# Projecting and rotating the keys of a batch element in one set of 128 rows, with their gap from a matmul and the first loads in another order

## The chip, the cores and the metric

The kernel runs on one core of a Trainium2 chip. The metric is the device time of one execution in microseconds, the median of three runs. One further execution was taken by the hardware profiler; all rows below come from it, with times from the start of its span.

## What is computed

One transformer layer over 4 batch elements of 1024 tokens and 256 features, in fp32: attention with 16 query heads and 4 key/value heads of 16 features, rotary embedding on queries and keys, then a gated feed-forward part, each with residual and layer norm. Only the start of it matters here:

```python
q = (hidden_states @ wq).reshape(B, S, H, D)
k = (hidden_states @ wk).reshape(B, S, Hkv, D)
v = (hidden_states @ wv).reshape(B, S, Hkv, D)
q = q * cos + _rotate_half(q) * sin
k = k * cos + _rotate_half(k) * sin
...
scores = jnp.einsum('bqkgd,bskd->bkgqs', qg, k) * scale
attn = jax.nn.softmax(scores, axis=-1)
```

## The kernel before

The five engines run programs written out by hand, ordered against each other by semaphores. There are three stages: projections, attention, feed-forward. The change is in the first.

**Projections.** The 4096 tokens are 8 blocks `m` of 512; two blocks make a batch element `b`, and `c` is the block within it. For each block TensorE (PE) runs six hooks `h`: two query halves `j` of two steps each (`project_q`, L1160, 128 output rows), and two steps for keys and values (`project_kv`, L1170). The block's 128 key/value rows are 64 of keys and 64 of values; which comes first alternates with `c`. One fp32 matmul appears in the trace as two instructions. VectorE (DVE) multiplies the query rows by the cosine and sine tables (L697, four products a block) and the key rows likewise (L705 to L707, three products of 64, 32 and 32 rows a block). GpSimd (POOL) adds or subtracts the products (`rotate`, L533). ScalarE (ACT) rounds each result to a high part (L959), and POOL, or DVE for the first query half of blocks 0 to 4, takes the rest as the low part (L522, L714). SyncE (SP) stores high and low parts in DRAM tensors `q_parts` and `k_parts`. For each batch element the difference of the rotated keys of its two blocks, the **gap**, is computed by DVE (L720) or, for the last two, POOL (L543), split the same way and stored too.

**Early maxima.** From block 5 on, PE adds in each hook two matmuls of the first attention unit (`max_block`, L1121), through a ring of PSUM banks: ACT takes one of a pair (L992, `above`) and DVE the other (L742). After block 7 the rest of them follows in a row. The row maxima of the first half unit are transposed by PE (`split`), split by DVE (L754, L756) and written by SP into `q_sb` (`load_shift`, L351); only then can the first scores (L1256) run.

**The queue of SP.** It is one ordered list. Inputs: `load_x(m)` loads block m of x. In block m SP waits for each high and low part before it stores it, and everything behind waits too. `load_x(m + 2)` stands after the two stores of the first query half of block m. `first_loads` (the operands of the first maxima, read back from DRAM) stands in block 3 behind the stores of that half, and first waits for all stores of batch element 0, its gap among them.

**The start.** SP issues x(0), wq, wkv (192 columns, since the key columns stand in it twice), both query tables whole, x(1), both key tables, x(2), the identity. PE waits for x(0), wq and wkv; DVE waits for all four tables.

Of the kernel before, what the change touches and what calls it, by code (L numbers as in the profile page):

```python
# [13 lines left out]
P = 128  # L14
CH = 512
# [23 lines left out]
GAPS = 2  # L39
# [5 lines left out]
QK = 3  # L45
PARTS = (3, 4, 7)
# [11 lines left out]
def layer(nc, x, xT, wq, wkv, wo, gate_w, gate_scale, up_w, up_scale, down_w, down_scale,  # L58
          cos, sin_q, cos_k, sin_k, identity, out):
    ctx = ExitStack()  # L60
    with ctx:
# [25 lines left out]
        wq_sb, wkv_sb = sb("wq_sb", [P, KE, E], fp32, one), sb("wkv_sb", [P, KE, 3 * HKV * D], fp32, one)  # L87
        cos_sb, sinq_sb = sb("cos_sb", [P, S], fp32, one), sb("sinq_sb", [P, S], fp32, one)
        cosk_sb, sink_sb = sb("cosk_sb", [P, CH], fp32, one), sb("sink_sb", [P, CH], fp32, one)
        by_cos = [sb(f"by_cos{c}", [P, CH], fp32, one) for c in range(QK)]  # L90
        by_sin = [sb(f"by_sin{c}", [P, CH], fp32, one) for c in range(QK)]
        v_rows = [sb(f"v_rows{c}", [P, CH], fp32, one) for c in range(2)]
        rotated = [sb(f"rotated{c}", [P, CH], fp32, one) for c in range(QK)]
        rotated_k = [rotated[QK - 1], sb("rotated_k1", [P, CH], fp32, one)]
        gap = sb("gap", [HKV * D, CH], fp32, one)
        gap_h, gap_l = sb("gap_h", [HKV * D, CH], f32r, one), sb("gap_l", [HKV * D, CH], f32r, one)
        high = [sb(f"high{c}", [P, CH], f32r, one) for c in range(2 * QK)]
        low = [sb(f"low{c}", [P, CH], f32r, one) for c in range(2 * QK)]
# [62 lines left out]
        kv_bank = [ring_bank[2], pv_bank]  # L161


        proj_loaded, consts_loaded = sem("proj_loaded"), sem("consts_loaded")
# [4 lines left out]
        lo_ready = [sem(f"lo_ready{j}") for j in range(QK)]  # L169
        stored = [sem(f"stored{c}") for c in range(2 * QK)]  # L170
        gap_ready, gap_h_ready, gap_l_ready, gap_stored = (sem(n) for n in ("gap_ready", "gap_h_ready", "gap_l_ready", "gap_stored"))
# [52 lines left out]
        for b in range(B):  # L224
            early[min(2 * b + 3, BLOCKS), 1].append(("v", b))
        for i in range(2 * LEAD):
            n, h = divmod(FIRST * HOOKS + i, HOOKS)
            where = early[(n, h) if n < BLOCKS else (BLOCKS, HOOKS - 1)]
            if i == 2 * KT + 1:
                where.append((0, "split"))  # L230
            where.extend(step(i))
        for n in range(BLOCKS + 1):
            if n == BLOCKS:
                wide_from = len(readers)
            for h in range(HOOKS):
                for key in early[n, h]:
                    place(key, "v" if key[0] == "v" else "max" if key[1] == "split" else ("above" if blocks(key[0], key[1] // 4)[key[1] % 4][1] == 2 else "max"))
# [20 lines left out]
        ring_taken = {"max": (ring_used, 1), "above": (above_ready, 1), "v": (v_used, 2)}  # L258
# [36 lines left out]
        def stores(slot):  # L295

            return 16 * 2

# [26 lines left out]
        def _(sp):  # L325
# [7 lines left out]

            load_x(0)
# [18 lines left out]
            def first_loads():  # L353

                for slot in range(2 * QK):
                    sp.wait_ge(stored[slot], stores(slot))
# [5 lines left out]
            def projections(b, first, last):  # L362
                for c in range(2):
                    cols = slice(c * CH, (c + 1) * CH)
                    for j in range(QK):
                        if j == 2 and c == 0 and not first:
                            store_gap(b - 1)
                        if j == 1 and 2 < 2 * b + c + 2 < BLOCKS:
                            load_x(2 * b + c + 2)
                        if b == 3 and c == 0 and j == 1:  # L370
                            load_kv(0, 0)
                            load_k(k_max, 0, 1, kmax_loaded, sp)
                            load_q(0, QH, sp)
                        if b == 1 and c == 1 and j == 1:
                            first_loads()
                        if b == 2 and c == 0 and j == 2:
                            load_q(0, 1, sp)
                        if last and c == 1 and j == 1:
                            load_shift(0, 0, taken_through((0, "split")))
                        slot = QK * c + j  # L380
                        for part, buf, ready, count in ((0, high, hi_ready, 2 * QK * b + slot + 1), (1, low, lo_ready[j], 2 * b + c + 1)):
                            sp.wait_ge(ready, count)
                            if j < 2:
                                dst = q_parts[H * b:H * (b + 1), part, j * HALF:(j + 1) * HALF, cols]
                                sp.dma_start(dst, buf[slot][:].bitcast(fp32)).then_inc(stored[slot], 16)
                            else:
                                store_k(part, b, cols, buf[slot], stored[slot])

            def store_k(part, b, cols, buf, done):
                dst = k_parts[b, part * D:(part + 1) * D, :, cols].rearrange("r h t -> (r h) t")  # L390
                sp.dma_start(dst, buf[0:HKV * D, :].bitcast(fp32)).then_inc(done, 16)

            def store_gap(b):
                for part, buf, ready in ((0, gap_h, gap_h_ready), (1, gap_l, gap_l_ready)):
                    sp.wait_ge(ready, b + 1)
                    store_k(part, b, slice(S, S + CH), buf, gap_stored)
# [32 lines left out]
            for slot in range(2 * QK):  # L429
                sp.wait_ge(stored[slot], stores(slot) * B)  # L430
# [75 lines left out]
        def _(pool):  # L506
# [9 lines left out]
            def low_part(n, slot, j, guard):  # L516
                rows = P if j < 2 else HKV * D
                if guard is not None:
                    pool.wait_ge(*guard)
                pool.wait_ge(hi_ready, n + 1)  # L520
                src = rotated[j] if j < 2 else rotated_k[slot // QK]
                pool.tensor_tensor(low[slot][0:rows], src[0:rows], high[slot][0:rows].bitcast(fp32), ALU.subtract).then_inc(lo_ready[j], 1)  # L522

            def rotate(m, j):
                b, c = divmod(m, 2)
                rows = P if j < 2 else HKV * D
                pool.wait_ge(parts_ready, PARTS[-1] * m + PARTS[j])
                if m:
                    pool.wait_ge(lo_ready[j], m if j < 2 else m - 1)
                if j == QK - 1 and b:  # L530
                    pool.wait_ge(gap_ready, b)
                dst = rotated[j] if j < 2 else rotated_k[c]
                pool.tensor_tensor(dst[0:rows], by_cos[j][0:rows], by_sin[j][0:rows], ALU.add if j else ALU.subtract).then_inc(rot_ready, 1)  # L533

            def low_of(m, j):
                b, c = divmod(m, 2)
                slot = QK * c + j
# [876 lines left out]
```

## Time and profile before

| | us |
|---|---|
| median of 3 runs (lowest to highest) | 948.05 (947.54 to 948.25) |
| the profiled execution's own time | 946.2 |
| its span | 944.0 |
| PE busy in the span | 909.5 (96%) |
| DVE busy | 761.7 (81%) |
| ACT busy | 720.3 (76%) |
| POOL busy | 263.1 (28%) |

The shares are averages over stages with different limits. The stage that is changed ends in the trace at the first scores, 91 us after the start.

### The profile page before, as it was taken

Reading aid. Unit: us, or ns where it says so; the run is one execution under the profiler, and the core shown is the slowest. Engines: PE = TensorE matmul, PEld = TensorE weight load, DVE = VectorE, ACT = ScalarE, POOL = GpSimd, SP = SyncE. Lnnn points to the kernel's source line nnn. Section 1 sums busy time; section 2 is a strip of 40 time slices with the busy share of each in tenths; the row PEclk is TensorE's granted clock in tenths of the full one; section 3 lists DMA queues with packets and bytes.
Section 4 is the critical chain, followed back from the end, with each engine's and each line's share of the span. In section 5 each row is a group of like instructions: output and inputs, shape, how many; then the busy total and the mean of one; then the engine's idle time right before and its main releaser. Section 6 shows DMA issues by size and latency. Waiting matters only on the chain.

```text
span 944.0 us, 15638 instructions
## 1 busy us (share of the span) xinstructions
PE 909.5 (96%) x5520; PEld 467.6 (50%) x5520; DVE 761.7 (81%) x1522; ACT 720.3 (76%) x938; POOL 263.1 (28%) x223
## 2 busy tenths in 40 slices
PE   7688999999999999999999999999999999999995
PEld 3234334344434444343434444444435888888884
DVE  4787899999999999999999999999973456655544
ACT  1356888989898898988998889888887555555564
POOL 5777366110001001001000100400101666656454
PEclk9797999999999999999999999999999999999998
DMA  6797633133131232213313123221110201101001
GB/s 206 205 266 199 140 89 93 44 85 72 44 72 45 58 76 69 51 43 74 82 45 68 49 51 84 68 52 42 33 52 14 69 24 46 45 26 42 24 23 47
DMA packets 44288, 68.85 MB, mean 73 GB/s; under 512 B 12592, under 2 KB 22832, under 8 KB 44208
## 3 DMA queue, kind: packets, MB, share of 16 engines
q1 hardware_dynamic: 43344, 64.67, 26.1%
q0 software_dynamic: 864, 3.15, 1.1%
q8 instruction: 46, 0.75, 0.3%
q14 instruction: 34, 0.28, 0.1%
HBM read 46.80 MB, written 16.25 MB: 67 GB/s over the span
## 4 chain that ended last, share of the span: by engine, by line
PE 86%; issue 4%; POOL 3%; DVE 2%; ACT 2%; DMA 1%; SPq 0%; POOLq 0%; DVEq 0%; ACTq 0%
PE pv_bank L1198 27%; PE ring_bank L1121 25%; PE pair_bank L1256 13%; PE pair_bank L1319 12%; PE pv_bank L1328 3%; PE ring_bank L1328 3%; PE ring_bank L1208 2%; POOL rotated L533 1%; POOL low L522 1%; ACT probs L1048 1%; PE ring_bank L1134 1%; PE ring_bank L1223 1%; POOL rotated_k L533 0%; DVE v_all L863 0%; DVE low L714 0%
## 5 line engine op out<-in xcount | busy, mean ns | idle before, releaser
L1048 ACT ACTIVATE probs<-pair_bank 128x1024 f32<-128x1024 f32 x512 | 496.4, 1026 | 68.2 <-PE pair_bank L1256 66.9
L745 DVE TENSOR_REDUCE block_max<-ring_bank 128x1 f32<-128x512 f32 x732 | 469.1, 683 | 33.3 <-PE ring_bank L1121 25.6
L1121 PE MATMUL ring_bank<-k_max,q_sb 48*128 48x512 f32 x1003 | 315.4, 476 | 4.6 <-DMA q_sb<-shift 2.2
L1198 PE MATMUL pv_bank<-probs,v_all 128*32 128x512 f32 x2048 | 273.6, 606 | 0.5 <-ACT probs L1048 0.5
L1121 PEld LDWEIGHTS ring_bank<-k_max,q_sb 48*128 48x128 f32 x1003 | 136.6, 185 | 252.1 <-DVE block_max L745 125.3
L1256 PE MATMUL pair_bank<-q_sb,k_sb 50*128 50x512 f32 x1024 | 204.4, 415 | 0.9 <-ACT probs L1048 0.9
L608 POOL TENSOR_TENSOR attn<-attn,inv_rows 128x1024 f32<-128x1024 f32 x7 | 16.7, 2379 | 489.2 <-DMA inv_rows<-inv_d 489.2
L906 DVE SCALAR_TENSOR_TENSOR hid<-pair_bank,up_s,silu 128x512 f32<-128x512 f32 x64 | 47.9, 748 | 86.7 <-ACT silu L1088 86.7
L1256 PEld LDWEIGHTS pair_bank<-q_sb,k_sb 50*128 50x128 f32 x1024 | 101.5, 187 | 32.8 <-ACT probs L1048 14.4
L650 POOL TENSOR_TENSOR hid_l<-hid,hid_h 128x512 fp32r<-128x512 f32 x64 | 82.9, 1295 | 87.8 <-ACT hid_h L1074 87.2
L742 DVE CUSTOM_DVE_ANT_0 above<-ring_bank,above 128x512 f32<-128x512 f32 x136 | 93.8, 692 | 10.5 <-ACT above L992 6.7
L992 ACT ACTIVATE above<-ring_bank 128x512 f32<-128x512 f32 x135 | 80.6, 599 | 6.5 <-PE ring_bank L1121 4.4
L1088 ACT ACTIVATE silu<-pair_bank,gate_s 128x512 f32<-128x512 f32 x64 | 43.7, 683 | 47.5 <-PE pair_bank L1319 47.3
L1198 PEld LDWEIGHTS pv_bank<-probs,v_all 128*32 128x32 f32 x2048 | 40.4, 108 | 74.0 <-issue 73.2
L1074 ACT ACTIVATE hid_h<-hid 128x512 fp32r<-128x512 f32 x64 | 40.3, 629 | 43.1 <-DVE hid L906 43.1
L1160 PE MATMUL pair_bank<-attn,wq_sb 128*128 128x512 f32 x64 | 38.4, 730 | 16.4 <-DMA attn<-xT 9.7
L1319 PE MATMUL pair_bank<-x1T_h,gate_h 128*128 128x512 f32 x128 | 41.1, 402 | 0.3 <-DVE hid L906 0.3
L1319 PE MATMUL pair_bank<-x1T_l,gate_h 128*128 128x512 f32 x128 | 40.5, 397 | 0.0
L1319 PE MATMUL pair_bank<-x1T_h,up_h 128*128 128x512 f32 x128 | 40.3, 396 | 0.0
L1319 PE MATMUL pair_bank<-x1T_l,up_h 128*128 128x512 f32 x128 | 40.3, 396 | 0.0
L959 ACT ACTIVATE high<-rotated 128x512 fp32r<-128x512 f32 (+1 forms) x20 | 12.6, 629 | 35.9 <-POOL rotated L533 35.9
L1328 PE MATMUL pv_bank<-down_h,hid_h 128*128 128x256 f32 x128 | 33.7, 284 | 1.9 <-POOL hid_l L650 1.6
(126 smaller groups left out, 873.4 us busy)
## 6 DMA issues: line engine op xcount, KB each, us to landing
q_sb<-q_parts SPq DMA_DIRECT2D x64, 128.0 KB, 3.3
k_max<-k_parts SPq DMA_DIRECT2D x32, 192.0 KB, 3.8
attn<-xT SPq DMA_DIRECT2D x8, 512.0 KB, 5.5
q_parts<-high SPq DMA_DIRECT2D x16, 256.0 KB, 3.5
q_parts<-low SPq DMA_DIRECT2D x16, 256.0 KB, 3.6
q_sb<-q_parts SPq DMA_DIRECT2D x64, 64.0 KB, 3.4
k_sb<-k_parts SPq DMA_DIRECT2D x32, 128.0 KB, 2.7
attn<-pv_sb SPq DMA_DIRECT2D x128, 32.0 KB
```

The costliest lines, as they stand in the source:

```text
L650: pool.tensor_tensor(hid_l[:, it, :], hid[it % 2][:], hid_h[:, it, :].bitcast(fp32), ALU.subtract).then_inc(hid_l_ready, 1)
L742: dve.tensor_tensor_reduce(out=buf[:], in0=bank, in1=buf[:], scale=1.0, scalar=-3.0e38, op0=ALU.add, op1=ALU.max, accum_out=block_max[half ...
L745: dve.reduce_max(block_max[half % 2][:, col:col + 1], bank, axis=AX.X).then_inc(ring_used, 1)
L906: dve.scalar_tensor_tensor(out=hid[it % 2][:], in0=pair_bank[it % 2][:, 1, :], scalar=up_s[:, it:it + 1], in1=silu[it % 2][:], op0=ALU.mul ...
L992: act.activation(above[(count - 1) % 2][:], bank_of(key), ACT.Relu).then_inc(above_ready, 1)
L1048: act.activation(probs[t % 2][:, 2 * pr:2 * pr + 2, :], pair_bank[pr][:], ACT.Exp, scale=D ** -0.5).then_inc(probs_ready, 1)
L1088: act.activation(silu[it % 2][:], pair_bank[it % 2][:, 0, :], ACT.Silu, scale=gate_s[:, it:it + 1]).then_inc(silu_ready, 1)
L1121: pe.matmul(bank, q_sb[k][rows, i, qt * P:(qt + 1) * P], k_max[k // QH][rows, kind * CH:(kind + 1) * CH], start=True, stop=True).then_inc( ...
L1198: ins = pe.matmul(pv_bank[32 * j:32 * j + 2 * D, :], v_all[:, head, t, :], probs[t % 2][:, 2 * (j % 2) + j // 2, :], start=(t == 0), stop= ...
L1256: ins = pe.matmul(pair_bank[pr][:, r, :], k_sb[s][rows, t * P:(t + 1) * P], q_sb[k][rows, pr, :], start=True, stop=True)
L1319: ins = pe.matmul(pair_bank[it % 2][:, u, :], w[:, k, it * P:(it + 1) * P], v[c][:, k, :], start=(q == 0), stop=(q == len(terms) - 1))
L1328: ins = pe.matmul(sum_bank[t // 2][:, (t % 2) * E:(t % 2 + 1) * E], v[:, k, t * P:(t + 1) * P], w[:, k, :], start=(k == 0 and t % 2 == 0 a ...
```

## The change

What it does:

- **Keys of a batch element in one bank.** `project_kv` now issues four matmuls of 32 output rows per step where one of 128 stood. The keys of both blocks of a batch element land in one bank of 128 rows (`k_bank`), the values of both in another (`v_bank`). Within a block the four strips go to the two banks in turn. DVE rotates the keys once per batch element (three products, of 128, 64 and 64 rows), POOL adds them once (`rotate_k`), ACT and POOL make one high and one low part of 128 rows, and SP stores them in four transfers per batch element of two x 32 rows, where it was two transfers per block. ACT copies the values once per batch element.
- **The gap by a matmul.** `key_signs`, +1 and -1 from the identity, multiplies the rotated keys on PE (`make_gap`, fp32, 64 output rows of 512) into a bank of the ring. ACT and DVE (always DVE now) split it from there. It stands in the last but one hook of the next batch element's first block, and for the last batch element behind the last early maximum.
- **Loads.** SP issues wq, x(0), the first half of both query tables, wkv (128 columns), the key tables, x(1), the second halves, x(2), the identity. PE waits at first for x(0) and wq only, DVE for each table at its first use. `load_x(m + 3)` stands where `load_x(m + 2)` stood, but x(5) comes behind `first_loads`, which moves from block 3 into block 2. The 12 loads of block 6 move ahead of that block's first stores.

```diff
-            load_x(0)
-            for dst, src in ((wq_sb, wq), (wkv_sb, wkv)):
-                sp.dma_start(dst[:], src.rearrange("(k p) n -> p k n", p=P)).then_inc(proj_loaded, 16)
-            for dst, src in ((cos_sb, cos), (sinq_sb, sin_q)):
-                sp.dma_start(dst[:], src).then_inc(consts_loaded, 16)
+            sp.dma_start(wq_sb[:], wq.rearrange("(k p) n -> p k n", p=P)).then_inc(wq_loaded, 16)
+            load_x(0)
+            load_q_tables(0)
+            sp.dma_start(wkv_sb[:], wkv.rearrange("(k p) n -> p k n", p=P)).then_inc(wkv_loaded, 16)
+            for dst, src in ((cosk_sb, cos_k), (sink_sb, sin_k)):
+                sp.dma_start(dst[:], src).then_inc(k_tables_loaded, 16)
             load_x(1)
-            for dst, src in ((cosk_sb, cos_k), (sink_sb, sin_k)):
-                sp.dma_start(dst[:], src).then_inc(consts_loaded, 16)
+            load_q_tables(1)
             load_x(2)
...
+            def projections(b, first, last):
+                for c in range(2):
+                    m = 2 * b + c
+                    if last and c == 0:
+                        load_kv(0, 0)
+                        load_k(k_max, 0, 1, kmax_loaded, sp)
+                        load_q(0, QH, sp)
+                    store_q(m, 0)
+                    if c == 0 and not first:
+                        store_gap(b - 1)
+                    if m + 3 < BLOCKS and m != 2:
+                        load_x(m + 3)
+                    if last and c == 1:
+                        load_shift(0, 0, taken_through((0, "split")))
+                    store_q(m, 1)
+                    if m == 2:
+                        first_loads()
+                        load_x(m + 3)
+                    if m == 4:
+                        load_q(0, 1, sp)
+                    if c == 1:
+                        store_k(b)
...
             def project_kv(m, k):
 
-                c = m % 2
-                if k == 0 and m > 1:
-                    pe.wait_ge(parts_ready, PARTS[-1] * (m - 1))
-                    pe.wait_ge(v_rows_ready, m - 1)
-                ins = pe.matmul(kv_bank[c][:], wkv_sb[:, k, HKV * D * c:HKV * D * (c + 2)], x_in[m][:, k, :], start=(k == 0), stop=(k == KE - 1))
+                b, c = divmod(m, 2)
+                if k == 0 and m == 0:
+                    pe.wait_ge(wkv_loaded, 16)
+                if k == 0 and c == 0 and b:
+                    pe.wait_ge(k_parts_ready, K_PARTS * b)
+                    pe.wait_ge(v_rows_ready, b)
+                for strip in range(4):
+                    a, other = strip // 2, strip % 2 != c
+                    col = (HKV * D if other else 0) + a * STRIP
+                    rows = slice(strip * STRIP, (strip + 1) * STRIP)
+                    ins = pe.matmul((v_bank if other else k_bank)[rows, :], wkv_sb[:, k, col:col + STRIP], x_in[m][:, k, :], start=(k == 0), stop=(k == KE - 1))
                 if k == KE - 1:
                     ins.then_inc(proj_ready, 1)
+
+            def make_gap(b):
+
+                pe.wait_ge(signs_ready, 1)
+                pe.wait_ge(k_rot_ready, b + 1)
+                bank = free_bank(("gap", b))
+                pe.matmul(bank[0:HKV * D, :], key_signs[:].rearrange("p a x -> p (a x)"), rotated_k[:], start=True, stop=True).then_inc(ring_ready, 1)
```

Three places in the order. The first is SP's queue behind the stores of the first gap, before the change; the `attn<-xT` in it is x(5).

```order
L391 DMA k_parts<-gap_h 64x512 [waits gap_h_ready]
L391 DMA k_parts<-gap_l 64x512 [waits gap_l_ready]
L391 DMA k_parts<-high2 64x512 [waits hi_ready]
L391 DMA k_parts<-low2 64x512 [waits lo_ready2]
L385 DMA q_parts<-high3 16x8x512 [waits hi_ready]
L385 DMA q_parts<-low3 16x8x512 [waits lo_ready0]
L332 DMA attn<-xT 128x2x512
L319 DMA k_max0<-k_parts 32x1536 [waits stored4,stored5,stored3,gap_stored,stored2,memsets,stored1,stored0]
L320 DMA k_max0<-k_parts 16x1536
```

The same place after the change, where the `attn<-xT` is again x(5).

```order
L395 DMA k_parts<-gap_l 64x512 [waits gap_l_ready]
L381 DMA q_parts<-high1 16x8x512 [waits hi_ready]
L381 DMA q_parts<-low1 16x8x512 [waits lo_ready1]
L324 DMA k_max0<-k_parts 32x1536 [waits k_stored0,stored3,gap_stored,stored2,memsets,stored1,stored0]
L325 DMA k_max0<-k_parts 16x1536
L324 DMA k_max0<-k_parts 32x1536
L325 DMA k_max0<-k_parts 16x1536
L315 DMA q_sb0<-q_parts 32x2x512
L316 DMA q_sb0<-q_parts 16x2x512
L315 DMA q_sb0<-q_parts 32x2x512
L316 DMA q_sb0<-q_parts 16x2x512
L337 DMA attn<-xT 128x2x512
```

x(5) stood ahead of the wait for the gap's store and of the eight loads; now it stands behind them, but all of it comes a block earlier.

The second place is PE's program at the end of the stage, before the change: the last two early maxima, the first two of the attention stage, and the first scores.

```order
L1121 MATMUL ring_bank<-k_max,q_sb 128x512 [waits above_ready]
L1121 MATMUL pair_bank<-k_max,q_sb 128x512 [waits above_ready]
L1121 MATMUL ring_bank<-k_max,q_sb 128x512 [waits shift_loaded0,memsets,kv_loaded0,v_used,parts_ready]
L1121 MATMUL ring_bank<-k_max,q_sb 128x512 [waits ring_used]
L1256 MATMUL pair_bank<-q_sb,k_sb 128x512 [waits ring_used]
```

And after the change.

```order
L1139 MATMUL ring_bank<-k_max,q_sb 128x512 [waits above_ready]
L1139 MATMUL pair_bank<-k_max,q_sb 128x512 [waits above_ready]
L1205 MATMUL pair_bank<-rotated_k,key_signs 64x512 [waits ring_used,k_rot_ready,signs_ready]
L1139 MATMUL ring_bank<-k_max,q_sb 128x512 [waits memsets,shift_loaded0,v_used,kv_loaded0,v_rows_ready,ring_used,k_parts_ready,parts_ready]
L1139 MATMUL ring_bank<-k_max,q_sb 128x512 [waits above_ready]
L1291 MATMUL pair_bank<-q_sb,k_sb 128x512 [waits gap_l_ready,ring_used]
```

The gap's matmul has come in ahead, and the first scores wait for DVE to have taken the gap's low part out of its bank.

## Rows read from the trace of the kernel before

**Rows 1.** The page's first line.

```profile
span 944.0 us, 15638 instructions
```

**Rows 2.** Busy time by stretch; engines, granted clock, DMA share, GB/s.

```profile
0.00:92.48 92.48, 70.39 (x170) 29.42 (x170) 65.36 (x120) 39.51 (x71) 66.05 (x57) 0.90 0.75 219
92.48:790.00 697.52, 695.79 (x4493) 311.83 (x4492) 612.18 (x1184) 595.87 (x722) 109.47 (x82) 1.00 0.25 62
...
40.00:50.00 10.00, 7.88 (x12) 3.13 (x12) 5.94 (x8) 2.06 (x5) 5.87 (x6) 0.68 0.97 262
```

**Rows 3.** Waits of PE up to 95 us: total, times, longest.

```profile
PE pair_bank L1160 <- DMA attn<-xT: 9.7, 3, 4.5
...
PE ring_bank L1121 <- DMA q_sb<-shift: 2.2, 1, 2.2
PE ring_bank L1121 <- DMA q_sb<-q_parts: 2.2, 1, 2.2
```

**Rows 4.** PE in order of time: start, duration, instruction, count, idle before.

```profile
6.72 6.46 PE L1160 MATMUL pair_bank<-attn,wq_sb 128*128 128x512 f32 x8 [6.72 <-DMA wkv_sb<-wkv]
13.01 1.88 PE L1170 MATMUL ring_bank<-attn,wkv_sb 128*128 128x512 f32 x4
...
41.43 6.17 PE L1160 MATMUL pair_bank<-attn,wq_sb 128*128 128x512 f32 x8 [4.34 <-DMA attn<-xT]
...
50.15 1.98 PE L1160 MATMUL pair_bank<-attn,wq_sb 128*128 128x512 f32 x4 [0.84 <-DMA attn<-xT]
...
61.14 1.12 PE L1160 MATMUL pair_bank<-attn,wq_sb 128*128 128x512 f32 x2
...
70.37 1.12 PE L1160 MATMUL pair_bank<-attn,wq_sb 128*128 128x512 f32 x2
71.85 1.12 PE L1160 MATMUL pair_bank<-attn,wq_sb 128*128 128x512 f32 x2
...
80.62 0.49 PE L1121 MATMUL pair_bank<-k_max,q_sb 48*128 48x512 f32 x1
```

**Rows 5.** DVE's and POOL's first work on the projections.

```profile
12.54 0.13 DVE L685 MEMSET block_max<- 128x32 f32 x2 [12.54 <-DMA sink_sb<-sin_k]
...
14.74 2.50 POOL L533 TENSOR_TENSOR rotated<-by_cos,by_sin 128x512 f32<-128x512 f32 x2 [8.17 <-DVE by_sin L697]
```

**Rows 6.** SP's queue in order of time.

```profile
44.18 0.59 SPq L332 DMA_DIRECT2D attn<-xT  x1
...
45.09 0.38 SPq L319 DMA_DIRECT2D k_max<-k_parts  x1
...
48.32 0.43 SPq L311 DMA_DIRECT2D q_sb<-q_parts  x1
```

**Rows 7.** DMA issues up to 60 us: count, size, from issue to landing.

```profile
attn<-xT SPq DMA_DIRECT2D x7, 512.0 KB, 5.4
...
wq_sb<-wq SPq DMA_DIRECT2D x1, 256.0 KB, 4.2
...
k_parts<-gap_l SPq DMA_DIRECT2D x2, 128.0 KB, 4.9
...
wkv_sb<-wkv SPq DMA_DIRECT2D x1, 192.0 KB, 4.9
```

**Rows 8.** The chain that ended last, in the attention stage.

```profile
99.02 0.99 PE pv_bank L1198 x8
```

**Rows 9.** ACT in block 7.

```profile
77.97 0.63 ACT L959 ACTIVATE high<-rotated 64x512 fp32r<-64x512 f32 x1 [2.03 <-POOL rotated L533]
```

**Rows 10.** SP, PE and DVE at the end of the stage.

```profile
86.20 2.87 SPq L351 DMA_DIRECT2D q_sb<-shift  x4
...
87.43 0.79 PE L1121 MATMUL pair_bank<-k_max,q_sb 48*128 48x512 f32 x1
...
89.06 0.69 DVE L742 CUSTOM_DVE_ANT_0 above<-pair_bank,above 128x512 f32<-128x512 f32 x1
...
91.00 0.66 PE L1256 MATMUL pair_bank<-q_sb,k_sb 50*128 50x512 f32 x2
```

More of the change, by code:

```diff
@@ L44 @@
 STORES = 16 * (G + 1)
-QK = 3
-PARTS = (3, 4, 7)
+Q_PARTS = 4
+K_PARTS = 3
+STRIP = HKV * HALF
+K_STORES = 2
 LAG = 2
@@ L224, in layer @@
         for b in range(B):
+            if b < B - 1:
+                early[2 * b + 2, HOOKS - 2].append(("gap", b))
             early[min(2 * b + 3, BLOCKS), 1].append(("v", b))
@@ L231, in layer @@
             where.extend(step(i))
+        early[BLOCKS, HOOKS - 1].append(("gap", B - 1))
         for n in range(BLOCKS + 1):
@@ L236, in layer @@
                 for key in early[n, h]:
-                    place(key, "v" if key[0] == "v" else "max" if key[1] == "split" else ("above" if blocks(key[0], key[1] // 4)[key[1] % 4][1] == 2 else "max"))
+                    place(key, key[0] if key[0] in ("v", "gap") else "max" if key[1] == "split" else ("above" if blocks(key[0], key[1] // 4)[key[1] % 4][1] == 2 else "max"))
         early_entries = len(readers)
@@ L360, in first_loads @@
                 load_q(0, 0, sp)
[L362 to L387, printed above, removed]
@@ L393, in store_gap, with store_k @@
+            def store_k(b):
+                for part, buf, ready in ((0, high_k, k_hi_ready), (1, low_k, k_lo_ready)):
+                    sp.wait_ge(ready, b + 1)
+                    for a in range(2):
+                        dst = k_parts[b, part * D + a * HALF:part * D + (a + 1) * HALF, :, 0:S].rearrange("r h (c t) -> c (r h) t", c=2)
+                        sp.dma_start(dst, buf[b % 2][a * 2 * STRIP:(a + 1) * 2 * STRIP, :].bitcast(fp32)).then_inc(k_stored[b % 2], 16)
             def store_gap(b):
@@ L514, in _ @@
             pool.wait_ge(memsets, 6)
[L516 to L522, printed above, removed]
             def rotate(m, j):
-                b, c = divmod(m, 2)
-                rows = P if j < 2 else HKV * D
-                pool.wait_ge(parts_ready, PARTS[-1] * m + PARTS[j])
+                pool.wait_ge(parts_ready, Q_PARTS * m + 3 + j)
@@ L528, in rotate @@
                 if m:
[L529 to L533, printed above, removed]
+                    pool.wait_ge(lo_ready[j], m)
+                pool.tensor_tensor(rotated[j][:], by_cos[j][:], by_sin[j][:], ALU.add if j else ALU.subtract).then_inc(rot_ready, 1)
@@ new lines, in low_of, with rotate_k @@
+                if b:
+                    pool.wait_ge(stored[slot], 16 * 2 * b)
+                pool.wait_ge(hi_ready, 2 * m + j + 1)
+                pool.tensor_tensor(low[slot][:], rotated[j][:], high[slot][:].bitcast(fp32), ALU.subtract).then_inc(lo_ready[j], 1)
+            def rotate_k(b):
+                pool.wait_ge(k_parts_ready, K_PARTS * (b + 1))
+                if b:
+                    pool.wait_ge(k_lo_ready, b)
+                    pool.wait_ge(ring_ready, places["gap", b - 1] + 1)
+                pool.tensor_tensor(rotated_k[:], by_cos[2][:], by_sin[2][:], ALU.add).then_inc(k_rot_ready, 1)
@@ L680, in _ @@
         def _(dve):
-            dve.wait_ge(consts_loaded, 16 * 4)
             for c in range(2):
@@ L761, in early_maxima @@
                         continue
+                    if key[0] == "gap":
+                        gap_low(key[1])
+                        continue
                     half, e = key
@@ L997, in early_takes @@
                         take_v(key[1])
+                    elif key[0] == "gap":
+                        gap_high(key[1])
                     elif key[1] != "split" and key[1] % 4 < 2:
@@ L1147, in early_work @@
                         transpose_v(key[1])
+                    elif key[0] == "gap":
+                        make_gap(key[1])
                     elif key[1] == "split":
```

226 lines of the change are left out of this document (119 added, 107 removed).

## The prediction

> **What bounds the kernel now.** I read the page first: PE is busy 96% of a span of 944.0 us [rows 1], so only time in which PE is idle or slow can be won. Busy time by stretch says where that is. From 92.5 to 790 us PE is busy 695.8 of 697.5 us at full clock; in the first 92.5 us it is busy 70.4 at a mean granted clock of 0.90 [rows 2]. The change touches the first stretch alone, so the question is when the first scores start: 91.0 us now [rows 10]. Behind that point the work is the same, and I carry its shift to the end at full value.
>
> The waits of PE say what is late in the first stretch: the blocks of x, 9.7 us in three waits [rows 3], because SP issues x(m+2) only behind stores of block m, which are the end of a chain PE, DVE, POOL, ACT, POOL. The waits cost more than themselves. After the 4.34 us idle before block 4, eight instructions took 6.17 us, while after 0.84 us idle four took 1.98 [rows 4]; the granted clock around the first was 0.68 [rows 2], so it fell to its lower level of 1.2 GHz for part of the time. That is some 2.4 us on one block. From block 5 on, projection steps come at 1.48 us (70.37 to 71.85), each with two maxima behind it, and PE sets the pace itself [rows 4]. At the end PE waits 2.2 us for the shift [rows 3].
>
> **The change, step by step**, as one clock run through the blocks.
>
> *Start.* PE waited until 6.72, for wkv, which took 4.9 us to land after wq's 4.2 [rows 4, 7]. wq was issued 0.5 us ahead of wkv, so it landed 1.2 us before it, at 5.5, with x(0) ahead of it in the queue. The same two transfers now lead, in the other order: PE starts at 5.5. Its eight cold instructions take 6.46 [rows 4]: 12.0. DVE no longer waits until 12.54 for the last key table [rows 5]; the tables that it needs at first are the next 512 KB in the queue. POOL's first rotation moves from 14.74 [rows 5] to about 12.7, two after DVE's first product of the second half.
>
> *Blocks 0 to 4.* A key/value step has four matmuls of 32 rows where one of 128 stood. The nearest row is the attention stage's 8 instructions of 32 rows in 0.99 us [rows 8]: four matmuls of this shape to the four strips, in the time of one. The old step took 1.88/2 = 0.94 [rows 4]. Those are the bounds of one side; the other is that strips to two banks in turn don't overlap, 4 x 0.86 = 3.44 a step. I take 0.99, since depth, shape, type and strips are the same and only the banks differ; the dearer one is a rival below. A block is then 3.44 + 2.0 = 5.4, the gap another 0.9. PE's blocks begin at 13.9, 19.3 and 25.6 (with a gap), 31.8 (with the value transposes), and block 4 ends at 38.2. POOL keeps up: 8 operations of 1.25 us [rows 5] per two blocks where there were 10, 10 us against PE's 12. x(3) and x(4) are issued about 16 and 23, and land 5.4 later [rows 7], before PE wants them at 25.6 and 31.8. So these two waits, 4.5 and 4.3 us, go.
>
> *The wait that is late next: x(5).* It now stands behind `first_loads`, and that behind the landing of the gap's stores. The chain: keys 0 rotated by POOL at 24.0, gap matmul to 25.6, ACT's high part behind its high part of query half (2,0), 26.8, DVE's low part 27.5; SP, some 0.6 us an issue and still busy with four key stores until 27.9, issues gap_l at 29.7. It lands 4.9 later [rows 7], at most 34.6; median stores would give 33.5. I take 34.2. The first of eight loads to the last took 45.09 to 48.75 [rows 6], 3.7 us, so x(5) is issued at 37.9 and lands at 43.6 (5.4 by the row, 6.0 in the run before, issued 44.18 and used at 50.15 [rows 4, 6]). PE idles 38.2 to 43.6, a new wait of 5.4 us that takes the place of the three old ones; behind it in PE's program is everything. Block 5 starts at 43.6 instead of 50.15: **-6.5**.
>
> *Block 5.* Before, 50.15 to 61.14, 11.0 us with the 2.2 us wait for q_sb [rows 3, 4]. That wait goes, since the eight loads are now issued ahead of x(5). Six steps at 1.48 are 8.9; strips add 0.3 (two steps, 0.99 for 0.86 of array time); the clock after 5.4 us idle costs about 2.6, as at block 4. 11.8: **+0.8**.
>
> *Block 6.* Before 9.2 (61.14 to 70.37) [rows 4]; now 8.9 + 0.3 + a gap matmul of 0.9, 10.1: **+0.9**. That gap costs its full time, as PE sets the pace; those of blocks 2 and 4 were hidden by the wait for x(5). DVE gives up three products a pair of blocks and takes a gap split, so it has room.
>
> *Block 7.* Before 10.25 to the row at 80.62 [rows 4]; the excess is one stall of about 1.1: ACT waits 2.03 us for a key rotation in POOL's queue, with PE's maxima behind it [rows 9]. That operation no longer stands there (keys are rotated after odd blocks only, and POOL runs 10 operations a pair from here on instead of 14). 8.9 x 5/6 + 0.6 for transposes + 1.1 + 0.3 = 9.4: **-0.85**.
>
> *The end.* Before, 80.62 to 91.00 is 10.4 us. The last link was the shift: DVE had it ready before, but SP, behind 12 loads and 8 stores, came to its four transfers at 86.20 only [rows 10], and PE waited 2.2 us [rows 3]. The loads now go out one wait earlier and SP is through in time; DVE's last early maximum, 89.06 + 0.69, would be next. But the gap has gone in behind it: PE's last maximum ends at 88.2 at the slow pace of 0.79 each, the gap takes 2 x 0.85 = 1.7 there, ACT 0.63, DVE 0.69 and two hand-overs: scores at 91.3 on the old clock. **+0.3**. Had the gap not come, this would be -1.2.
>
> Sum: -6.5 + 0.8 + 0.9 - 0.85 + 0.3 = -5.4. The profiled execution took 946.2, 1.9 below the median, so span 944.0 becomes 938.6 and the median 948.05 becomes **942.7 us**.
>
> One rule of the Trainium skill speaks against the strips: "TensorEngine Tiling (Array Packing)", Key Properties, says that a change of tiling mode drains TensorE, and each new step is two such changes between matmuls of 128 columns. The attention stage makes the same changes around its groups of eight, and its 0.99 against 0.86 holds them [rows 8]. "TensorE: Matmul & The Clock Gate", "Why this matters for your kernels", gives 2.38 times for three such strips, not three times; a step would then be an estimated 1.08 us, and the sum 943.2.
>
> **The rivals.**
>
> *Slower: strips to alternating banks don't overlap.* The row that shows overlap has one bank. A step of 3.44 adds 2.45; ten steps in blocks 0 to 4 add 24.5, of which 5.4 is hidden in the wait for x(5), six more add 14.7: 34 us, less 5.4 won, about 976. It decides from 5.4 + 5.4 = 10.8 us over 16 steps, 0.7 each, a step of 1.7 us. For it: nothing in the trace has two banks. 8%.
>
> *Smaller gain, or none: x(5) is later.* It hangs on one chain through five engines and on transfers that share a DMA already 0.97 busy [rows 2]. Three us late, with the clock low for block 5, gives 945.7; five gives 947.7. 20%, half of them within 0.2% or near it.
>
> *Larger gain.* ACT and DVE, not PE, held blocks 6 and 7 more than I think, or the stores land sooner and the clock holds through block 5 (-2.6): 940. 13%.
>
> *The forecast*, 941 to 945.5: 53%. A remaining 6% is for waits I don't see, of either sign.
>
> **The numbers.** 0.2% is 1.9 us, about what the measurement tells from no change. Faster: forecast, larger, half of the smaller, some of the rest, 79%. Same 10%, slower 11%. The range of 939.5 to 947.3 leaves out the rival of 976, the ends of the late x(5), and gains above 8.5.
>
> **What would show it.** PE's first instruction at 5.5; no wait for x(3) or x(4); one wait for x(5) of about 5.4 us that ends near 43.6, low clock behind it; eight strip instructions in about 1.0 us; no wait for q_sb; first scores near 85.6, released by DVE's gap low part and not by the shift. A strip step of over 1.7, or x(5) after 48, makes me wrong.

## The result, and the profile after

The changed kernel takes **958.31 us** (median; 954.78 to 961.71) where the kernel before takes 947.79: a ratio of 1.0107, 95% interval 1.0083 to 1.013. That is slower by 1%, above the range of 939.5 to 947.3 and of the other sign than the forecast of 942.7. The traced execution, from which the rows below come, took 954.78, the least of the four; what the others lost beyond it (3.5 us at the median) is in no trace.

The page after shows PE busy 914.5 us, 5 more than before, and idle 38.5 us of 953.0, where it was busy 909.5 and idle 34.5 of 944.0.

```profile
span 953.0 us, 15805 instructions
...
PE 914.5 (96%) x5624; PEld 465.6 (49%) x5624; DVE 749.8 (79%) x1511; ACT 715.5 (75%) x930; POOL 247.9 (26%) x211
```

The waits of PE up to 100 us (total, times, longest) are what answers to [rows 3]. The three waits for x have become one of 14.2, beside the 5.5 at the start that falls under the same name.

```profile
PE pair_bank L1180 <- DMA attn<-xT: 19.7, 2, 14.2
PE ring_bank L1139 <- DMA q_sb<-shift: 2.1, 1, 2.1
```

PE in order of time, against [rows 4, 10]: the start, a block's first key/value steps (L1196; a row per instruction, of which the first of each of two steps stands here) and the start of the next block, the first gap, block 5, the last gap and the first scores.

```profile
5.47 6.32 PE L1180 MATMUL pair_bank<-attn,wq_sb 128*128 128x512 f32 x8 [5.47 <-DMA attn<-xT]
11.72 0.62 PE L1196 MATMUL ring_bank<-attn,wkv_sb 128*32 128x512 f32 x1
...
12.60 0.59 PE L1196 MATMUL ring_bank<-attn,wkv_sb 128*32 128x512 f32 x1
...
13.57 3.70 PE L1180 MATMUL pair_bank<-attn,wq_sb 128*128 128x512 f32 x8
...
24.54 1.07 PE L1205 MATMUL ring_bank<-rotated_k,key_signs 128*64 128x512 f32 x2
...
52.40 3.78 PE L1180 MATMUL pair_bank<-attn,wq_sb 128*128 128x512 f32 x4 [14.19 <-DMA attn<-xT]
...
90.65 1.97 PE L1205 MATMUL pair_bank<-rotated_k,key_signs 128*64 128x512 f32 x2
94.69 0.79 PE L1139 MATMUL ring_bank<-k_max,q_sb 48*128 48x512 f32 x2 [2.08 <-DMA q_sb<-shift]
95.26 0.66 PE L1291 MATMUL pair_bank<-q_sb,k_sb 50*128 50x512 f32 x2
```

All goes as forecast up to 52.40 less 14.19, which is 38.2, the end of block 4: start, strips, gap, no wait for x(3) or x(4). Then x(5) comes at 52.40 instead of 43.6. The first scores start at 95.26, 4.3 us later than before [rows 10]; the span is 9.0 us longer, so another 4.7 us go after that point.

SP's queue (start, time that the issue took) says why x(5) is late. x(5) itself is the `attn<-xT` at 46.82.

```profile
25.60 1.55 SPq L389 DMA_DIRECT2D k_parts<-high_k  x2
27.55 1.52 SPq L389 DMA_DIRECT2D k_parts<-low_k  x2
29.12 3.98 SPq L381 DMA_DIRECT2D q_parts<-high  x1
...
33.79 1.23 SPq L395 DMA_DIRECT2D k_parts<-gap_h  x1
35.06 0.92 SPq L395 DMA_DIRECT2D k_parts<-gap_l  x1
...
43.16 0.36 SPq L324 DMA_DIRECT2D k_max<-k_parts  x1
...
46.82 0.42 SPq L337 DMA_DIRECT2D attn<-xT  x1
```

The four key stores (L389) are issued by 29.1, and the store behind them, an ordinary one, is stuck 3.98 us in its own issue. gap_l goes out at 35.06 where 29.7 was forecast. In the chain of work that ended last it then takes 7.94 us to land, not 4.9:

```profile
35.06 7.94 DMA k_parts<-gap_l
...
46.82 5.54 DMA attn<-xT
```

gap_l is only the last that the first loads wait for. The first, SP's own waits show, was the landing of the key stores' low part:

```profile
SPq L368 <- DMA k_parts<-low_k: 3.2, 1, 3.2
SPq L369 <- DMA k_parts<-gap_l: 1.9, 1, 1.9
```

SP is through with its issues at 37.9 (36.69 + 1.20), waits for low_k until 41.1 and for gap_l until 43.0. The last key store was issued by 29.1, so it is 12 us until all four have landed. Without the slow gap_l the loads would still have been held until 41.1.

The stretches behind the key stores, in the columns of [rows 2]; the last but one is the share of the 16 DMA engines that is busy.

```profile
29.00:30.00 1.00, 1.00 (x6) 0.16 (x8) 1.00 (x3) 0.96 (x3) 0.44 (x1) 1.00 0.18 37
31.00:32.00 1.00, 1.00 (x9) 0.30 (x2) 1.00 (x3) 0.00 (x0) 0.81 (x1) 1.00 0.12 33
32.00:33.00 1.00, 1.00 (x4) 0.52 (x3) 0.97 (x2) 0.51 (x1) 1.00 (x2) 1.00 0.13 45
...
42.00:43.00 1.00, 0.00 (x0) 0.00 (x0) 0.00 (x0) 0.57 (x1) 0.00 (x0) 0.50 0.13 49
```

0.12 and 0.13 are what two busy engines of sixteen give (0.125), at 33 to 49 GB/s. SP is held up while the DMA is nearly empty. The kernel before has shares of 0.94, 0.46, 0.58 and 0.89 from 29 to 33 us; its stretch from 31 us:

```profile
31.00:32.00 1.00, 1.00 (x2) 0.42 (x2) 0.97 (x2) 0.51 (x2) 0.93 (x1) 0.50 0.58 123
```

What is different about these stores is `store_k`: its DRAM side is `"r h (c t) -> c (r h) t"`, an outer dimension of two with 32 rows in each, where the old stores, one per block, had 64 rows as outer dimension. The stretch from 42 us shows the share of two engines again just before gap_l lands at 43.0. That would fit gap_l's part on those two queued behind the key stores; the profile doesn't say which engines carry which store.

The Trainium skill has this rule in "DMA: Bandwidth & Descriptors", section "Why a DMA increments its semaphore by 16 and not by 1": a transfer is spread over the largest number of engines, up to 16, that divides the slowest dimension of both its sides. By that rule, 2 for these stores, the trace agrees (share 0.12 to 0.13).

### The profile page after: what moved, and what is told of

It is laid out like the page before. It is cut to its first block, busy times and chain, and to the rows that moved or that the text cites. A ratio compares the mean times of both kernels' runs of the same rounds, so it can differ in the third digit from the quotient of the medians.

```text
span 953.0 us, 15805 instructions
## 1 busy us (share of the span) xinstructions
PE 914.5 (96%) x5624; PEld 465.6 (49%) x5624; DVE 749.8 (79%) x1511; ACT 715.5 (75%) x930; POOL 247.9 (26%) x211
## 4 chain that ended last, share of the span: by engine, by line
PE 88%; DMA 3%; DVE 2%; ACT 2%; SPq 2%; POOL 1%; issue 1%; POOLq 0%; DVEq 0%
PE pv_bank L1233 26%; PE ring_bank L1139 25%; PE pair_bank L1291 13%; PE pair_bank L1354 11%; PE pv_bank L1363 3%; PE ring_bank L1363 3%; PE pair_bank L1180 2%; PE ring_bank L1243 2%; DMA attn<-xT 1%; DMA k_parts<-gap_l 1%; ACT probs L1066 1%; POOL rotated L544 1%; DVE block_max L757 1%; PE ring_bank L1258 1%; PE ring_bank L1152 1%
## 5 line engine op out<-in xcount | busy, mean ns | idle before, releaser
L1291 PEld LDWEIGHTS pair_bank<-q_sb,k_sb 50*128 50x128 f32 x1024 | 102.1, 187 | 32.7 <-ACT probs L1066 14.2
L1354 PE MATMUL pair_bank<-x1T_h,gate_h 128*128 128x512 f32 x128 | 41.1, 402 | 0.4 <-DVE hid L923 0.4
L1363 PE MATMUL ring_bank<-down_h,hid_h 128*128 128x256 f32 x128 | 33.5, 283 | 0.0
```

The lines of the kernel that those rows point to most:

```text
L1291: ins = pe.matmul(pair_bank[pr][:, r, :], k_sb[s][rows, t * P:(t + 1) * P], q_sb[k][rows, pr, :], start=True, stop=True)
L1354: ins = pe.matmul(pair_bank[it % 2][:, u, :], w[:, k, it * P:(it + 1) * P], v[c][:, k, :], start=(q == 0), stop=(q == len(terms) - 1))
L1363: ins = pe.matmul(sum_bank[t // 2][:, (t % 2) * E:(t % 2 + 1) * E], v[:, k, t * P:(t + 1) * P], w[:, k, :], start=(k == 0 and t % 2 == 0 a ...
```

## The experiments

Three theories at first. **A**: the shape of the key stores slows them and what is queued behind them. **B**: the order does it, since x(5) stands behind the wait for the gap and the eight first loads. **C**: SP has too much to issue, so that more and smaller stores make it worse. Every kernel was timed in rounds beside the kernel before, whose medians lay at 947.79, 947.22, 947.40 and 947.16 us in the four batches, the changed kernel's first; so times of different batches may be compared to about 0.6 us.

| kernel | median (lowest to highest), us | ratio to before, 95% |
|---|---|---|
| keys32 | 941.95 (939.75 to 944.63) | 0.993 [0.9905, 0.9955] |
| x5_first | 956.89 (954.84 to 958.92) | 1.0106 [1.0074, 1.0138] |
| keys32_x5 | 938.07 (937.4 to 938.71) | 0.9901 [0.9878, 0.9924] |
| spare2 | 964.51 (963.23 to 965.96) | 1.0184 [1.0152, 1.0216] |
| spare64 | 950.19 (948.2 to 951.84) | 1.0023 [1.001, 1.0036] |
| spare4 | 953.04 (952.75 to 954.27) | 1.0063 [1.0046, 1.008] |
| loads_only | 946.5 (944.59 to 951.66) | 0.9993 [0.9978, 1.0008] |
| keys32_oldx | 944.25 (941.72 to 945.24) | 0.9963 [0.9948, 0.9979] |
| gap_early | 938.57 (937.65 to 943.18) | 0.9912 [0.9891, 0.9932] |
| k0_2x32 | 944.31 (943.44 to 949.11) | 0.9971 [0.996, 0.9981] |
| k3_2x32 | 944.69 (943.34 to 946.81) | 0.9971 [0.9955, 0.9987] |

### keys32: the same kernel, each key store cut into two of 32 rows

```diff
-                    for a in range(2):
-                        dst = k_parts[b, part * D + a * HALF:part * D + (a + 1) * HALF, :, 0:S].rearrange("r h (c t) -> c (r h) t", c=2)
-                        sp.dma_start(dst, buf[b % 2][a * 2 * STRIP:(a + 1) * 2 * STRIP, :].bitcast(fp32)).then_inc(k_stored[b % 2], 16)
+                    for s in range(4):
+                        a, c = divmod(s, 2)
+                        dst = k_parts[b, part * D + a * HALF:part * D + (a + 1) * HALF, :, c * CH:(c + 1) * CH].rearrange("r h t -> (r h) t")
+                        sp.dma_start(dst, buf[b % 2][s * STRIP:(s + 1) * STRIP, :].bitcast(fp32)).then_inc(k_stored[b % 2], 16)
```

> The changed kernel, but each key store of 2 x 32 rows is issued as two stores of 32 rows (eight a batch element instead of four, same bytes). Theory A, the shape of the stores: with an outer dimension of 2 a store runs on 2 of the 16 DMA engines, and everything that shares those two engines lands late, x(5) above all. Then the DMA share of 0.12 to 0.18 between 29 and 33 us is gone, gap_l lands some 5 us after its issue instead of 7.9, x(5) near 44 instead of 52.4, the first scores near 86 to 88 instead of 95.3, and the time is 942 to 946. Theory B, the order: x(5) behind the first loads is the cause, and the shape of the stores costs nothing: 956 to 959, as the changed kernel. Theory C, SP itself: four more issues a batch element make it later: 959 or more.

941.95 us, 16.4 less than the changed kernel. The same data goes out in eight transfers per batch element instead of four, and it is faster: theory C falls, and B, which had 956 to 959. SP no longer waits for low_k, only 1.4 us for gap_l. The DMA share in the stretches that showed 0.12 to 0.18 is now 0.32 to 0.60:

```profile
29.00:30.00 1.00, 1.00 (x6) 0.18 (x9) 1.00 (x3) 1.00 (x3) 0.29 (x1) 1.00 0.60 203
30.00:31.00 1.00, 1.00 (x12) 0.26 (x8) 1.00 (x3) 0.12 (x1) 1.00 (x1) 1.00 0.32 82
31.00:32.00 1.00, 1.00 (x9) 0.30 (x2) 1.00 (x3) 0.00 (x0) 0.68 (x2) 1.00 0.58 148
32.00:33.00 1.00, 1.00 (x3) 0.38 (x2) 0.97 (x2) 0.36 (x1) 1.00 (x2) 1.00 0.58 133
```

And PE: x(5) at 46.16 after 7.81 us idle, the first scores at 87.91, no wait for the shift. x(5) is 2 us later than I expected (near 44).

```profile
46.16 3.78 PE L1181 MATMUL pair_bank<-attn,wq_sb 128*128 128x512 f32 x4 [7.81 <-DMA attn<-xT]
...
87.91 0.80 PE L1292 MATMUL pair_bank<-q_sb,k_sb 50*128 50x512 f32 x2 [0.82 <-DVE gap_l L737]
```

### x5_first: the changed kernel, with x(5) ahead of the first loads

```diff
-                    if m + 3 < BLOCKS and m != 2:
+                    if m + 3 < BLOCKS:
                         load_x(m + 3)
...
                     if m == 2:
                         first_loads()
-                        load_x(m + 3)
```

> The changed kernel, but x(5) is issued behind the gap's stores of block 2, ahead of the first loads. Key stores as in the changed kernel. Theory A (the shape of the stores): the first loads still wait for the key and gap stores that land late, and PE's first maximum waits for them; x(5) comes some us earlier, but PE only goes one step further before it waits for q_sb: 953 to 958. Theory B (the order): the wait for x(5) goes, 944 to 948.

956.89 us: theory B falls as the cause. PE still waits 11.1 us in two waits for x (5.8 the longest), then 2.6 for the queries of the first maxima and 5.0 for the shift. Moving x(5) only moves the wait to what else lies behind the key stores.

### keys32_x5: both edits

> Both edits together. Theory A: x(5) in time and the first loads as in the run with 32-row stores; PE waits for q_sb at about 43 instead of for x(5) at 44, so 0 to 2 us less than the run with 32-row stores alone: 940 to 945. Theory B: 944 to 948, the same as with x(5) moved alone. Theory C: 956 or more.

938.07 us, the best version of the study, 1% faster than before, and below the 940 to 945 that theory A gave. Against x5_first it is 18.8 us less: the shape of the stores again. Against keys32 it is 3.9 us less, so with the stores mended the order of x(5) does matter. PE's waits up to 100 us:

```profile
PE pair_bank L1180 <- DMA attn<-xT: 5.0, 1, 5.0
PE ring_bank L1139 <- DMA q_sb<-q_parts: 4.6, 1, 4.6
PE pair_bank L1291 <- DVE gap_l L736: 0.8, 1, 0.8
```

The wait of 5.0 is the start's; x(5) is in time, and the queries of the first maxima hold PE for 4.6 us, until 43.05.

### spare2, spare64, spare4: extra stores in the kernel before

The kernel before, with one more store behind each of its 16 key stores, 128 KB from the same tile to a DRAM tensor that nothing reads. The kernels add these 16 stores and leave nothing out. Only the shape of the DRAM side differs; the gap between the groups keeps them apart.

```diff
+        spare = nc.dram_tensor("spare", (B, 2, 2, 2, 40, CH), fp32).ap()
...
                                 store_k(part, b, cols, buf[slot], stored[slot])
+                                sp.dma_start(spare[b, c, part, :, 0:32], buf[slot][0:HKV * D, :].bitcast(fp32)).then_inc(stored[slot], 16)
```

This is spare2, two groups of 32 rows. spare64 writes `spare[b, c, part].rearrange("a x t -> (a x) t")[0:64]`, 64 rows in one; spare4 has a tensor of `(B, 2, 2, 4, 20, CH)` and writes `spare[b, c, part, :, 0:16]`, four groups of 16 rows.

> The kernel before, with one more store of the same 64 key rows behind each key store, into an unused tensor whose rows lie in two groups with a hole between them (2 x 32 x 512, 128 KB, 16 of them, read by nothing). Theory A: these too run on 2 of 16 engines and hold up the x blocks behind them; against the same stores to an unbroken tensor of 64 rows, sent later in the same way, it is slower by 5 us or more: 955 or more. Theories B and C: the same as with the unbroken tensor, 948 to 951.

> The control of the run with stores of 2 x 32 rows: the kernel before with the same 16 spare stores at the same places, but to an unbroken tensor of 64 rows. Theory A (an outer dimension of 2 puts a store on 2 of 16 DMA engines): these cost little, one or two issues on SP a block and 128 KB each: 948 to 952, against 964.5. Theory C (number of issues on SP and bytes): 960 or more, as with 2 x 32 rows.

> The kernel before with the same 16 spare stores of 64 rows, now to a tensor in four groups with holes (4 x 16 x 512). Theory A: the outer dimension sets how many DMA engines carry a store, here 4 of 16, each with half the bytes of the run with 2 x 32 rows: 953 to 958, between 950.2 (64 rows unbroken) and 964.5. If instead any broken-up tensor takes a slow path, it is like 2 x 32 rows, 962 or more.

Unbroken, the 2 MB of extra writes take 950.19 us, some 3 us over before. In four groups they take 953.04, in two groups 964.51: the same bytes, 2.9 and 14.3 us dearer. The tensor of four groups has holes too, so it isn't the holes alone. The stretches from 22 to 26 us, behind the first such store, first of spare2, then of spare4, then of spare64:

```profile
22.00:24.00 2.00, 1.73 (x5) 0.42 (x3) 1.65 (x3) 0.59 (x1) 2.00 (x2) 1.00 0.37 76
24.00:26.00 2.00, 0.00 (x0) 0.00 (x0) 1.07 (x2) 1.11 (x2) 1.26 (x2) 1.00 0.37 81
```

```profile
22.00:24.00 2.00, 1.79 (x5) 0.48 (x3) 1.08 (x2) 0.00 (x0) 2.00 (x2) 1.00 0.50 111
24.00:26.00 2.00, 0.00 (x0) 0.00 (x0) 1.67 (x3) 1.22 (x2) 1.26 (x2) 1.00 0.79 205
```

```profile
22.00:24.00 2.00, 2.00 (x6) 0.76 (x4) 1.76 (x3) 0.63 (x1) 2.00 (x3) 1.00 0.67 154
24.00:26.00 2.00, 0.55 (x2) 0.00 (x0) 0.96 (x2) 1.00 (x2) 1.26 (x2) 1.00 0.73 157
```

From 22 to 24 us the two-group kernel has the emptiest DMA, 0.37 against 0.50 (four groups) and 0.67 (unbroken); from 24 to 26 it alone stays there (0.37, 0.79, 0.73). SP's issues show the same: behind the first two spare stores, an ordinary one takes 2.24 us in spare2 and then another 2.72, x takes 1.80 in spare4, and in spare64 nothing takes over 0.61.

```profile
24.86 2.24 SPq L386 DMA_DIRECT2D q_parts<-low  x1
```

In spare2 PE's waits for x are 25.0 us in five (longest 10.9), in spare4 15.3 in three (7.9), in spare64 13.3 in three (6.5). So the cost belongs to the shape, not to strips, gap matmul or order: none of these is in the three kernels.

### k0_2x32 and k3_2x32: the old shape for one batch element only

keys32_x5, with the stores of batch element 0, or of 3, as in the changed kernel (k3_2x32 has `b == 3` below).

```diff
                     sp.wait_ge(ready, b + 1)
+                    if b == 0:
+                        for a in range(2):
+                            dst = k_parts[b, part * D + a * HALF:part * D + (a + 1) * HALF, :, 0:S].rearrange("r h (c t) -> c (r h) t", c=2)
+                            sp.dma_start(dst, buf[b % 2][a * 2 * STRIP:(a + 1) * 2 * STRIP, :].bitcast(fp32)).then_inc(k_stored[b % 2], 32)
+                        continue
```

> The version with 32-row key stores and x(5) first, with the stores of batch element 0 alone in the form of the change (2 x 32 rows, four instead of eight). Theory A: the first loads wait for these stores, so PE's wait for q_sb ends some 5 us later: 942 to 946 against 938.1.

> The same version with the stores of batch element 3 alone in the form of the change. Theory A: they hold up what SP issues at the start of attention, and the shift of the second half unit lands late, as in the changed kernel (3 us idle around 117 us and a lower clock behind it): 941 to 944 against 938.1. If the loss behind the first scores has another cause, 938.

944.31 and 944.69 us, 6.2 and 6.6 more than keys32_x5. Batch element 0's stores bring the wait for x(5) back (6.6 us), in a trace whose execution is the slowest of its ten (949.11). Those of element 3 are issued from 82.98 only, and hurt behind the first scores: from there to the end of the span it is 859.7 us against 853.3. The first scores themselves come at 85.11 against 82.34, but those 2.8 us are there before these stores, in a slower start (the first eight instructions 5.98 us against 5.07) and in a lower clock from 50 to 55 us (0.58 against 1.00); they are the execution's, not the edit's. 944.69 lies a little above the expected 944. SP's queue of k3_2x32:

```profile
82.98 1.08 SPq L390 DMA_DIRECT2D k_parts<-high_k  x2
84.11 1.55 SPq L390 DMA_DIRECT2D k_parts<-low_k  x2
85.70 3.73 SPq L428 DMA_DIRECT2D wo_sb<-wo  x1
...
99.29 0.33 SPq L315 DMA_DIRECT2D q_sb<-q_parts  x1
...
103.97 2.12 SPq L362 DMA_DIRECT2D q_sb<-shift  x3
```

In keys32_x5 the load at 99.29 is issued at 89.08 and the second shift at 97.23. Here PE waits 2.7 us for that shift in the attention stage, and from 110 to 120 us its granted clock is 0.55. The changed kernel has the same: the issue of `wo` takes 3.74 us where it took 0.59 before, the load comes at 111.27 (96.91 before), the shift at 114.91 (105.77 before), and PE waits. The issue of `wo` after, then before, and PE's wait after:

```profile
96.74 3.74 SPq L423 DMA_DIRECT2D wo_sb<-wo  x1
...
91.66 0.59 SPq L401 DMA_DIRECT2D wo_sb<-wo  x1
...
119.60 0.50 PE L1139 MATMUL ring_bank<-k_max,q_sb 48*128 48x512 f32 x2 [3.03 <-DMA q_sb<-shift]
```

The ten us from 20 us behind the first scores, after and before:

```profile
115.26:125.26 10.00, 6.97 (x43) 2.49 (x40) 5.38 (x10) 5.82 (x8) 6.76 (x4) 0.83 0.74 161
...
111.00:121.00 10.00, 10.00 (x69) 4.08 (x72) 9.23 (x18) 9.39 (x12) 4.10 (x3) 1.00 0.71 133
```

PE is busy 6.97 of the 10 us at a clock of 0.83, where before it was busy all of them at 1.00. The wait of 3.03 and the clock (by estimate 10 times 0.17, 1.7 us) make up the 4.7 us that went behind the first scores. The stores of the elements 1 and 2 weren't tried alone; 18.8 less 6.2 and 6.6 leaves 6.0 for them, if the costs add.

### loads_only and keys32_oldx: the loads alone, and the keys with the old order of the loads

loads_only is the kernel before with the new order at the start, the split waits for the tables, and x(m+3); its keys, gap, first loads and the 12 loads of block 6 are as before. keys32_oldx is keys32 with `load_x(m + 2)` and the first loads in block 3, as before; it keeps the new order at the start.

Of loads_only, on the kernel before:

```diff
-                        if j == 1 and 2 < 2 * b + c + 2 < BLOCKS:
-                            load_x(2 * b + c + 2)
+                        if j == 1 and 2 * b + c + 3 < BLOCKS:
+                            load_x(2 * b + c + 3)
```

And keys32_oldx, on keys32:

```diff
-                    if m + 3 < BLOCKS and m != 2:
-                        load_x(m + 3)
+                    if 2 < m + 2 < BLOCKS:
+                        load_x(m + 2)
+                    if m == 3:
+                        first_loads()
```

> The kernel before with the new order and waits of the first loads and with x(m + 3) where x(m + 2) stood, x(5) included; keys, gap and first loads as before. Theory D, the loads make the gain of the good version: PE starts at 5.5, the waits for x go, the first loads come some 4 us earlier: 942 to 945. Theory E, the gain needs the merged keys, since POOL's and DVE's chain of five operations a block holds the first loads anyway: 946 or more.

> The changed kernel with 32-row key stores, but x(m + 2) in block m and the first loads in block 3, as before the change; the start as in the changed kernel. Theory D: PE waits for x(3), x(4) and for q_sb again: 944 to 948. Theory E: the merged keys carry the gain: 939 to 942.

loads_only gains nothing that can be told: 946.5, as theory E had it. Only one wait for x is left, the start's 5.5 us, but PE then waits for DVE's products of a block's keys, and for the first loads, which still stand in block 3:

```profile
34.50 3.78 PE L1170 MATMUL pair_bank<-attn,wq_sb 128*128 128x512 f32 x4 [4.65 <-DVE by_sin L705]
...
51.92 0.79 PE L1131 MATMUL ring_bank<-k_max,q_sb 48*128 48x512 f32 x1 [9.78 <-DMA q_sb<-q_parts]
```

keys32_oldx, the keys and the new start without the earlier x and first loads, gives 944.25, 0.4% of the 1%; that is in the range of theory D and not of E, which had 939 to 942. So neither theory holds alone. Together the two give 938.07.

### gap_early: the last gap's matmul two steps earlier

keys32_x5 with the last gap placed ahead of two of the last early maxima. In the table of PE's order:

```diff
-        early[BLOCKS, HOOKS - 1].append(("gap", B - 1))
+        early[BLOCKS, HOOKS - 1].insert(-5, ("gap", B - 1))
```

> The version with 32-row key stores and x(5) first, and the last gap's matmul two early steps (four maxima, one of them behind it in its pair) further up instead of behind the last early maximum. If the last gap is what releases the first scores, as predicted, they come 0.8 to 1.5 us earlier and the time is 936.5 to 937.5 against 938.1. If ACT and DVE are full there in any case, no difference.

938.57 against 938.07, and the 0.8 to 1.5 us that I expected aren't seen. The intervals, some 0.2% to each side, are too wide to rule them out; the trace says it better. From the end of the last key/value step to the first scores it has 11.4 us (72.19 to 83.55), keys32_x5 11.0 (71.31 to 82.34). The wait for gap_l went, but the maxima behind the gap now wait for ACT (1.26 us), and the two instructions of the gap take as long as before:

```profile
77.90 1.97 PE L1205 MATMUL pair_bank<-rotated_k,key_signs 128*64 128x512 f32 x2
...
82.71 0.80 PE L1139 MATMUL ring_bank<-k_max,q_sb 48*128 48x512 f32 x2 [1.26 <-ACT above L1011]
83.55 0.79 PE L1291 MATMUL pair_bank<-q_sb,k_sb 50*128 50x512 f32 x2
```

## Why the prediction was wrong

**The step that failed** is *the wait that is late next: x(5)*. There I wrote "SP, some 0.6 us an issue and still busy with four key stores until 27.9, issues gap_l at 29.7. It lands 4.9 later". Both numbers took the four new transfers of "two x 32 rows" for ordinary ones; their shape was in the change's description and cost nothing in the sum. Measured: the key stores are issued until 29.1, the next issue takes 3.98 us, gap_l goes at 35.06 (5.4 late) and lands in 7.9 (3.0 more; with the 0.4 by which I took the landing shorter than its row, x(5) is 8.8 late, 52.40 for 43.6). The step also let the loads wait for the gap's stores alone, where low_k of batch element 0, issued by 29.1 and landed by 41.1, would have held them 7 us past the forecast 34.2 by itself. The rival "x(5) is later" had the place right and its size wrong: three or five us were priced, from a busy DMA, and the DMA was nearly empty from 29 to 33 us. keys32 and the spare kernels show the cause. keys32 also changes the number of stores and the rows of each; between spare2 and spare64 the groups of the DRAM side alone differ.

**The end** failed by the same cause. I had "SP is through in time" and 10.7 us from the last projection to the first scores. Measured, 82.86 to 95.26, 12.4, with 2.1 us of waiting for the shift that I had struck out (SP comes to it at 89.85 only, behind query stores that take up to 1.54 us to issue). With 32-row stores that wait is gone and the scores are released by DVE's low part of the gap, as forecast (0.82 us).

**"I carry its shift to the end at full value"** failed too: the first scores came 4.3 us later, the span 9.0. The last key stores lie ahead of the attention stage's first loads in SP's queue, and k3_2x32 shows that they alone cost 6.6 us, behind the first scores. In the trace the miss of 14.4 us on the span (953.0 for 938.6) is so 8.8 for x(5), less 0.8 won in blocks 5 to 7, 1.7 for the end and 4.7 behind it.

**Confirmed**, in the trace of the changed kernel:
- The start: 5.47 for 5.5. No wait for x(3) or x(4), and block 4 ends at 38.2 as forecast.
- The strips: a step of 0.88 us (11.72 to 12.60) and, with the start of the next matmul, 0.97 (12.60 to 13.57), for 0.99. Between early maxima it is 0.99 (70.17 to 71.16), where the old step took 1.05 (67.41 to 68.46 before). So the 0.3 us a block that I added for strips in blocks 5 to 7 was mis-sized: they cost nothing there and give back 0.1. Strips to two banks overlap, and the rival of 976 us is out. A price of the change of tiling mode that I weighed against them is not to be seen: between the maxima the step with its two changes is no longer than the one without.
- The eight loads 3.66 us for 3.7, x(5)'s landing 5.5 for 5.7.
- Block 5 11.55 for 11.8, the low clock behind the wait included; block 6 10.07 for 10.1, with its gap matmul (1.0 us for 0.9; the last one, at the lower clock, 1.9 for 1.7); block 7 8.84 for 9.4.

From x(5) to the first scores I had 42.0 us (43.6 to 85.6); keys32 takes 41.75 (46.16 to 87.91). Its median of 941.95 lies beside the forecast of 942.7. That close a fit is partly luck: in its trace x(5) is still 2.6 us late (high_k's four issues took 4.46 us), in an execution that is the slowest of its eight, 944.63.

**What the whole change is worth** without the fault of the stores is 0.7% (keys32), and 1% with x(5) ahead of the first loads (keys32_x5). It takes both halves: with the earlier loads alone PE waits for DVE and the first maxima instead, with the merged keys and the old order for x (13.2 us in four waits, the start's 5.2 among them).

## What to carry to other kernels

Read the outer dimension of both sides of every transfer that a change rewrites, before counting bytes or issues: fewer, larger transfers with two groups on the outside cost 16 us here against twice as many plain ones. In the profile the sign is a DMA share of some 2/16 while SP's next issue takes microseconds; PE's waits never name the store, only what is queued behind it; SP's own waits do (low_k, 3.2 us). And a late item in SP's queue is to be followed past the stage that is changed, to the loads of the next stage.

## What the runs showed of the hardware

- Stores of 128 KB whose DRAM side has 2 groups of 32 rows kept the DMA at a share of 0.12 to 0.18 and 33 to 49 GB/s; with four of them in a row, the last to land did so 12 us after the last was issued. 16 of them cost 14.3 us over the same bytes as 64 rows, 16 with 4 groups 2.9 us.
- The queue pushes back: the issue of an ordinary 256 KB store behind four such stores took SP 3.98 us where it is some 0.6 in the kernel before, that of `wo` 3.74 us where it was 0.59. Plain 32-row stores aren't free of it: the first four of keys32 took 4.46 us together, in keys32_x5 2.82.
- Four fp32 matmuls of 32 rows to two banks in turn take 0.88 to 0.99 us a step, the time of about one of 128 rows (0.94 [rows 4], 1.05 between early maxima).
- An fp32 matmul of 64 rows by 512 takes 1.07 us (two instructions) at the full clock and 1.97 at the lower one. The last gap ran at the lower one in both places tried (granted clock 0.50), and moving it bought nothing.
